# Attention over the heads of a token: groups of 32 tokens at a step of four instead of eight neighbours

## The chip, the cores and the metric

The kernel runs on one core of a Trainium2 chip. The metric is the device time of one launch in microseconds (us), the median of several runs. Lower is better. Engines are called as in the profile: PE (matrix products; PEld is its weight load), DVE (vector), ACT (activations), POOL, and SP, which here only issues transfers. Each engine works through its own list of instructions in order and waits on semaphores.

## The reference

One layer over x of shape (2, 4096, 512), in float32, with two halves that are both residual.

```python
h = layernorm(x);  k = h @ Wk.T;  r = h @ Wr.T
y = wkv_scan(-exp(time_decay), time_first, k, r)      # a recurrence over the 4096 tokens
x = x + (sigmoid(r) * y) @ Wo.T
z = layernorm(x)                                      # the feed-forward half works on z
h = rmsnorm(z, gamma1)
q = (h @ Wq + bq).reshape(b, t, 16, 32)
k, v = split(((h @ Wdown + bdown) @ Wup + bup).reshape(b, t, 16, 64))
att = softmax(einsum('bthd,btgd->bthg', q, k) / sqrt(32))   # 16 x 16 for each token
z = z + einsum('bthg,btgd->bthd', att, v).reshape(b, t, 512) @ Wo + bo
h2 = rmsnorm(z, gamma2);  gate = softmax(h2 @ Wg + bg)      # 8 experts, all of them used
x = x + z + einsum('btd,edf,bte->btf', h2, We, gate)
```

The attention here is unusual: it runs over the 16 heads within one token, not over tokens. Each token has a 16 x 16 matrix of scores of its own.

## The kernel before

**Tiles and stages.** The tokens are worked through in 32 tiles of T = 256. Four stages run at once on different tiles: "pre" (load and normalise tile i + 1), "mix" (the recurrence, tile i), "att" (the attention, tile i - 1) and "moe" (the experts, tile i - 2). One iteration runs a step of each. The order of the steps is a list written out by hand, `ORDER`, and each engine takes from it the steps in which it has work, in that order. Waits between engines are semaphore counts, kept in tables (`Steps`).

**Numbers.** A float32 operand is split into two float16 halves, "hi" and "lo", and a product is three float16 passes. For q and k, ACT makes the value and its hi half (`heads`, L595 and L598), POOL the lo half (`lo_half`, L476).

**Groups.** A matmul computes the scores of eight tokens at once: a group of NJ = 8 tokens gives 128 columns, 16 heads by 8 tokens. There are G = 32 groups in a tile. In the product of the group's q with its k only those entries count in which both columns belong to one token. Rows of a mask, added to the contraction, push the other entries far down, so that an exponential makes them zero.

**The stack.** For this product the parts of q and k are stacked along the partitions: 32 rows of head channels for each of three hi/lo pairings, eight mask rows, and in qs two more rows for the maximum (hi and lo). qs and ks have the shape [128, 32 groups, 4, 32] in float16: within a group 4 head blocks f by (4 blocks b times 8 tokens j). qo16 and k16 hold the 16 heads as 128 partitions (4 blocks f of 32) by 4 blocks b, so stacking moves data between partitions. SP does most of it by transfers inside the SBUF (L413, L417 in `att_up`): eight for q hi, four for q lo, four for k lo, of 32 partitions by 32 groups by 64 bytes each. DVE copies the two k hi parts in eight copies (L943 in `att_stack`).

```python
sp.dma_start(dst[n * HD:(n + 1) * HD, :, f, :],
             grouped(src, 0)[f * HD:(f + 1) * HD].rearrange("p g b j -> p g (b j)"))
```

**The steps around it, in `ORDER`.** `att_up` (K and V products, L1165; DVE writes V at L935), the recurrence's decay, `att_stack`, MoE step 2, `att_vt` (a transpose of V, L949), MoE 3, `att_max` (for each four groups four matmuls, L1182, and one reduce, L954, into four columns of mcol), with MoE 4 and 5 between, then `att_m`: the maxima, one per row of a group's matrix. They are needed as a row of the stack, so DVE turns mcol by a 32 x 32 block transpose (L959), makes hi and lo in m16 (L961, L799), and SP sends m16 in eight transfers into two rows of qs (L424): four for hi, four for lo, of 32 partitions by 64 bytes each.

```python
for l, step in enumerate(("m_hi", "m_lo")):
    sp.wait_ge(*att_dve.done(t, step))
    for f in range(F):
        sp.dma_start(qs[SCAN_ROWS + l:SCAN_ROWS + l + 1, :, f, :], m16[f * G:(f + 1) * G, l, :])
```

MoE 6 and 7 and half of the recurrence's end stand between this and `att_scores` (L1191), which waits on PE for all eight. ACT exponentiates (L608), `att_probs` multiplies by V (L1201), DVE divides. `att_back` turns the result back by one DVE transpose of 1,024 columns (L975), ACT and DVE split it (L614, L799), and after MoE 12 and 13 PE multiplies it by Wo (`att_project`).

Of the kernel before, what the change touches and what calls it, by code (L numbers as in the profile page):

```python
# [33 lines left out]
HF = CB // 2  # L34
F = H // CB
XS = 2048.0
NEG_INF = -1e38
# [111 lines left out]
def build(nc, x, wk, wr, wo1, decay, first, gamma1, wq, bq, wdown, bdown, wup, bup, wo2, bo, gamma2,  # L149
          wg, bg, we, ident_in, kmask_in, qmask_in, out):  # L150
    with ExitStack() as ctx:
# [61 lines left out]
        vp = sb("vp", [P, G, HD + 1])  # L213
        qs, ks = sb("qs", [P, G, F, CB * NJ], F16), sb("ks", [P, G, F, CB * NJ], F16)
        pr = sb("pr", [P, 2, 4 * P])
        mcol, mturn, m16 = sb("mcol", [P, G]), sb("mturn", [P, CB * NJ]), sb("m16", [P, 2, CB * NJ], F16)
        rden = sb("rden", [P, G])
# [13 lines left out]
        def grouped(split16, half_):  # L231

            return split16[:, half_, :, :].rearrange("p b t -> p (b t)").rearrange("p (g b j) -> p g b j", g=G, b=CB)

        def as_f32(flat):
            return flat.bitcast(F32).rearrange("p (b c) -> p b c", c=C)

        home = {"k": [as_f32(qs[:, :, :, :].rearrange("p g f x -> p (g f x)"))],
                "r": [as_f32(ks[:, :, :, :].rearrange("p g f x -> p (g f x)"))]}
        for name, after in zip(BIG[2:], BIG[3:]):  # L240
# [18 lines left out]
        def turned(n):  # L259
# [12 lines left out]
        stack_in = Steps(sem("stack_in"), 16, qk=16)  # L272
        m_in = Steps(sem("m_in"), 16, m=2 * F)
        stored = Steps(sem("stored"), 16, out=1)
# [14 lines left out]
        att_dve = Steps(sem("att_dve"), stats=2, idle=1, aggr=2, var=2, h=2, h_lo=2, xn=2, c_lo=1, v=4, stack=8,  # L289
                        vt=1, smax=8, m_turn=1, m_hi=1, m_lo=1, norm=16, ot=1, ot_lo=2, x2=2, h2=2, h2_lo=2)  # L290
        gate_dve = Steps(sem("gate_dve"), gl=1, gmax=1, gsub=1, gsum=1, grec=1, gmul=1, gates=1)
# [64 lines left out]
        def _(sp):  # L356
# [28 lines left out]
            def rest():  # L385

                for e in range(E):
                    load_weight(f"e{e}")
                sp.wait_ge(lo_done, split_done("r"))
                sp.dma_start(ks[3 * HD:SCAN_ROWS + 2, :, :, :], kmask_in.rearrange("a (g f x) -> a g f x", f=F, g=G)).then_inc(masks_in, 16)  # L390
                sp.dma_start(qs[3 * HD:SCAN_ROWS, :, :, :], qmask_in.rearrange("a (g f x) -> a g f x", f=F, g=G)).then_inc(masks_in, 16)

# [11 lines left out]
            def att_up(t, _):  # L404


                for src, dst, name, first in ((qo16, qs, "q", (0, 1)), (k16, ks, "k", ())):
                    rest = 2 if first else 1
                    for f in range(4):
                        for n in first:  # L410
                            if f == 0 and n == 0:
                                sp.wait_ge(*att_act.done(t, name))
                            sp.dma_start(dst[n * HD:(n + 1) * HD, :, f, :],  # L413
                                         grouped(src, 0)[f * HD:(f + 1) * HD].rearrange("p g b j -> p g (b j)")).then_inc(stack_in.sem, 16)
                    sp.wait_ge(*att_pool.done(t, f"{name}_lo"))
                    for f in range(4):
                        sp.dma_start(dst[rest * HD:(rest + 1) * HD, :, f, :],  # L417
                                     grouped(src, 1)[f * HD:(f + 1) * HD].rearrange("p g b j -> p g (b j)")).then_inc(stack_in.sem, 16)

            def att_m(t, _):  # L420
                for l, step in enumerate(("m_hi", "m_lo")):
                    sp.wait_ge(*att_dve.done(t, step))
                    for f in range(F):
                        sp.dma_start(qs[SCAN_ROWS + l:SCAN_ROWS + l + 1, :, f, :], m16[f * G:(f + 1) * G, l, :]).then_inc(m_in.sem, 16)  # L424

# [9 lines left out]
        def _(pool):  # L435
# [37 lines left out]
            def lo_half(t, step, dst):  # L473
                for b in range(CB):
                    pool.wait_ge(*att_act.done(t, step, 2 * b + 1))
                    nc.gpsimd.tensor_tensor(grouped(dst, 1)[:, :, b, :], t32[:, b % 2, :].rearrange("p (g j) -> p g j", g=G),  # L476
                                            grouped(dst, 0)[:, :, b, :], ALU.subtract).then_inc(att_pool.sem, 1)
# [27 lines left out]
        def _(act):  # L505
# [81 lines left out]
            def heads(t, use, step, dst, scale, bias, lo, before):  # L587

                for b in range(CB):
                    act.wait_ge(*att_pe.done(t, f"{use}{b // 2}"))  # L590
                    if b >= 2:
                        act.wait_ge(*att_pool.done(t, lo, b - 2))
                    elif before:
                        act.wait_ge(*att_pool.done(t, before, b + 2))
                    nc.scalar.activation(t32[:, b % 2, :], att_bank[ATT_BANK[use, b // 2]][:, (b % 2) * T:(b % 2) * T + T],  # L595
                                         ACT.Identity, bias=bias[:, b:b + 1], scale=scale).then_inc(att_act.sem, 1)
                    act.wait_ge(*att_act.done(t, step, 2 * b))
                    nc.scalar.activation(grouped(dst, 0)[:, :, b, :], t32[:, b % 2, :].rearrange("p (g j) -> p g j", g=G), ACT.Copy)\  # L598
                        .then_inc(att_act.sem, 1)
# [44 lines left out]
        def _(dve):  # L644
# [293 lines left out]
            def att_stack(t, _):  # L938

                dve.wait_ge(*att_act.done(t, "k"))  # L940
                for f in range(4):
                    for n in (0, 2):
                        V.tensor_copy(ks[n * HD:(n + 1) * HD, :, f, :],  # L943
                                      grouped(k16, 0)[f * HD:(f + 1) * HD].rearrange("p g b j -> p g (b j)")).then_inc(att_dve.sem, 1)

# [94 lines left out]
        def _(pe):  # L1040
# [234 lines left out]
```

## Time and profile before

| | |
|---|---|
| median of 3 runs | 3334.51 us (3332.51 to 3334.67) |
| profiled execution, its own time | 3332.17 us |
| profiled execution, span of the trace | 3330.3 us |
| PE busy | 2887.2 us, 87% |
| DVE busy | 2476.6 us, 74% |
| ACT busy | 956.6 us, 29% |
| POOL busy | 686.1 us, 21% |
| transfers | 588,333 packets, 102.96 MB; 556,562 under 512 bytes |

The span is what the trace covers, the time of the execution lies 1.9 us above it. Busy time is an average over all stages, so it doesn't tell where an engine sets the pace. In the rows below, a row of the timeline gives start, duration, engine, line, operation, what is written and read, and in brackets how long the engine had been idle and what ended it.

### The profile page before, as it was taken

What the parts mean: (1) busy time and instruction counts of PE and PEld (TensorE: products, weight loads), DVE (VectorE), ACT (ScalarE), POOL (GpSimd) and SP (SyncE); (2) the same over time, 40 slices, a digit from 0 to 9 for tenths busy, and PEclk for the clock granted to TensorE, in tenths of its full rate; (3) what the DMA queues carried; (4) which work ended last, traced back from release to release, by engine and by line L of the source; (5) the groups of instructions that cost most, each with busy time, mean ns of one, the idle gap of its engine ahead of it and who ended that gap; (6) DMA issues with size and microseconds to landing.
All of it is one profiled execution on the core that took longest, in us unless ns stands there. A gap on an engine that the chain in (4) does not pass through costs nothing.

```text
span 3330.3 us, 53600 instructions
## 1 busy us (share of the span) xinstructions
PE 2887.2 (87%) x18864; PEld 1791.2 (54%) x18864; DVE 2476.6 (74%) x4548; ACT 956.6 (29%) x1823; POOL 686.1 (21%) x745
## 2 busy tenths in 40 slices
PE   2359999998888989989998898999889998999889
PEld 2235555554555655555564555555555555555544
DVE  5797777778777768777777777768777777877753
ACT  2243232322332322322331332232233232232320
POOL 0111222212122212222221222221222221212210
PEclk9669999999999999999999999999999999999999
DMA  6011111101111101111111111111111110111110
GB/s 192 15 24 20 33 33 26 30 24 33 20 33 27 33 20 33 20 33 26 33 27 26 20 33 30 29 26 27 27 26 33 27 33 20 32 21 33 26 20 13
DMA packets 588333, 102.96 MB, mean 31 GB/s; under 512 B 556562, under 2 KB 556690, under 8 KB 588050
## 3 DMA queue, kind: packets, MB, share of 16 engines
q1 hardware_dynamic: 588068, 99.40, 16.4%
q8 instruction: 170, 2.79, 0.4%
q14 instruction: 95, 0.78, 0.1%
HBM read 48.49 MB, written 16.78 MB: 20 GB/s over the span
## 4 chain that ended last, share of the span: by engine, by line
PE 62%; DVE 23%; issue 7%; SPq 5%; DMA 2%; ACT 0%; POOL 0%; DVEq 0%; ACTq 0%; POOLq 0%
PE bank L1049 49%; PE bank L1201 6%; DVE mcol L954 4%; SPq L424 4%; DVE zz L865 3%; PE bank L1079 3%; DVE ks L943 3%; DVE wkv L839 2%; PE bank L1191 2%; DMA qs<-m 2%; DVE acc L1028 1%; DVE wkv L827 1%; PE bank L1165 1%; DVE ht L935 1%; DVE zz L832 1%
## 5 line engine op out<-in xcount | busy, mean ns | idle before, releaser
L1049 PE MATMUL bank<-w_e,h2t 128*128 128x512 f16 x6144 | 1479.4, 398 | 19.1 <-DVE acc L1028 19.1
L1049 PEld LDWEIGHTS bank<-w_e,h2t 128*128 128x128 f16 x6144 | 617.9, 103 | 757.5 <-issue 123.1
L1028 DVE SCALAR_TENSOR_TENSOR acc<-bank,gates,acc 128x512 f32<-128x512 f32 x512 | 373.6, 737 | 164.7 <-PE bank L1049 163.6
L1201 PEld LDWEIGHTS bank<-vp,pr 128*128 128x128 f32 x2048 | 263.9, 197 | 24.0 <-DVE hrow L970 3.9
L1201 PE MATMUL bank<-vp,pr 128*128 128x33 f32 x2048 | 259.7, 275 | 3.8 <-ACT pr L608 2.7
L608 ACT ACTIVATE pr<-bank,col 128x512 f32<-128x512 f32 x256 | 171.9, 685 | 316.1 <-PE bank L1191 315.7
L865 DVE RECIPROCAL zz<-zz 128x256 f32<-128x256 f32 x128 | 219.1, 1733 | 46.8 <-POOL zz L462 46.8
L1049 PE MATMUL bank<-w_o,xo 128*128 128x512 f16 x768 | 174.3, 384 | 58.8 <-DVE xo L799 58.8
L455 POOL TENSOR_TENSOR e<-wkv 128x512 f32<-128x512 f32 x64 | 72.1, 1127 | 645.6 <-DVE wkv L827 645.6
L1191 PE MATMUL bank<-qs,ks 106*128 106x128 f16 x1024 | 104.5, 236 | 113.9 <-DMA qs<-m 113.9
L1182 PE MATMUL bank<-ks,qs 104*128 104x128 f16 x1024 | 90.8, 231 | 125.7 <-DMA ks<-k 65.7
L935 DVE TENSOR_SCALAR ht<-bank,col,bvcol 128x256 f32<-128x256 f32 x128 | 61.8, 539 | 162.2 <-PE bank L1165 162.2
L1049 PE MATMUL bank<-w_o,qo 128*128 128x512 f16 x768 | 173.6, 383 | 4.4 <-DVE qo L799 4.4
L1049 PE MATMUL bank<-xo,w_k 128*128 128x256 f16 x1536 | 174.4, 274 | 0.0
L1049 PE MATMUL bank<-xo,w_r 128*128 128x256 f16 x1536 | 172.9, 273 | 0.0
L1049 PE MATMUL bank<-ht,w_q 128*128 128x256 f16 x1536 | 172.9, 273 | 0.0
L487 POOL TENSOR_TENSOR ve<-msq,eps_rms 128x2 f32<-128x2 f32 x32 | 6.3, 196 | 767.6 <-ACT hrow L620 767.6
L1049 PEld LDWEIGHTS bank<-xo,w_k 128*128 128x128 f16 x1536 | 151.0, 98 | 18.0 <-DVE xo L799 0.2
L1049 PEld LDWEIGHTS bank<-xo,w_r 128*128 128x128 f16 x1536 | 150.3, 98 | 17.4
L1049 PEld LDWEIGHTS bank<-ht,w_q 128*128 128x128 f16 x1536 | 150.2, 98 | 17.5
L954 DVE TENSOR_REDUCE mcol<-bank 128x4 f32<-128x512 f32 x256 | 158.4, 681 | 1.4 <-PE bank L1182 1.4
L462 POOL TENSOR_TENSOR zz<-wkv,zz 128x512 f32<-128x512 f32 x64 | 80.9, 1264 | 359.6 <-DVE wkv L839 359.6
(177 smaller groups left out, 3918.1 us busy)
## 6 DMA issues: line engine op xcount, KB each, us to landing
qs<-qo SPq DMA_DIRECT2D x384, 64.0 KB, 3.0
xk<-in_attn_x SPq DMA_DIRECT2D x32, 512.0 KB, 3.9
x<-in_attn_x SPq DMA_DIRECT2D x32, 512.0 KB, 3.6
result<-acc SPq DMA_DIRECT2D x32, 512.0 KB, 2.8
ks<-k SPq DMA_DIRECT2D x128, 64.0 KB, 3.0
w_e<-in_ffn_We SPq DMA_DIRECT2D x7, 1024.0 KB, 13.8
qs<-m SPq DMA_DIRECT2D x256, 2.0 KB, 1.7
qs<-in_attn_Wk SPq DMA_DIRECT2D x1, 1024.0 KB, 5.5
```

What stands on the lines that cost most here:

```text
L424: sp.dma_start(qs[SCAN_ROWS + l:SCAN_ROWS + l + 1, :, f, :], m16[f * G:(f + 1) * G, l, :]).then_inc(m_in.sem, 16)
L608: nc.scalar.activation(pr[:, k % 2, :], att_bank[ATT_BANK["S", k]][:, :], ACT.Exp, scale=colof["soft"])\
L865: V.reciprocal(zz[:, c, :], zz[:, c, :]).then_inc(mix_dve.sem, 1)
L935: V.tensor_scalar(va32[:, :, b, :], att_bank[ATT_BANK["V", b // 2]][:, (b % 2) * T:(b % 2) * T + T] .rearrange("p (g j) -> p g j", g=G), c ...
L943: V.tensor_copy(ks[n * HD:(n + 1) * HD, :, f, :], grouped(k16, 0)[f * HD:(f + 1) * HD].rearrange("p g b j -> p g (b j)")).then_inc(att_dve ...
L954: V.tensor_reduce(mcol[:, 4 * k:4 * k + 4], att_bank[ATT_BANK["M", k]][:, :].rearrange("p (g x) -> p g x", g=4), AX, ALU.max).then_inc(att ...
L1028: V.scalar_tensor_tensor(out=acc[:, s, :], in0=moe_bank[u % 2][:, :], scalar=gates[:, s, e:e + 1], in1=acc[:, s, :], op0=ALU.mult, op1=ALU ...
L1049: ins = nc.tensor.matmul(dst, left(a), right(b), start=(n == 0), stop=(n == last))
L1079: ins = nc.tensor.transpose(banks[b][:, c * T + s * P:c * T + (s + 1) * P], rows_[:, s, (2 * b + c) * P:(2 * b + c + 1) * P], ident[:, :])
L1182: ins = nc.tensor.matmul(att_bank[ATT_BANK["M", k]][:, n * P:(n + 1) * P], group(qs, SCAN_ROWS, 4 * k + n), group(ks, SCAN_ROWS, 4 * k + n ...
L1191: ins = nc.tensor.matmul(att_bank[ATT_BANK["S", k]][:, n * P:(n + 1) * P], group(ks, SCAN_ROWS + 2, 4 * k + n), group(qs, SCAN_ROWS + 2, 4 ...
L1201: ins = nc.tensor.matmul(att_bank[ATT_BANK["PV", k]][:, n * (HD + 1):(n + 1) * (HD + 1)], pr[:, k % 2, n * P:(n + 1) * P], vp[:, 4 * k + n ...
```

## The change

A group now takes every fourth token of 32 instead of eight neighbours. The groups come in GQ = 8 blocks of 32 tokens, R = 4 groups to a block; token t is in block t // 32, and its group within the block is t % 4. qs and ks get the shape [128, 8 blocks, 4, 32, 4], in which the group's number within its block is the last index. So 32 neighbouring tokens of a block b lie together: a transfer for the stack writes 256 bytes at once, and DVE copies runs of 128 elements. A group's columns are then no longer neighbours: PE reads every fourth column of the stack (for weights and for moving data). The V product reads its tokens in the new order too, so that everything behind it is laid out as before up to `att_back`, whose transpose becomes four, with the results written four elements apart. For the maxima the four groups of a block stand next to each other in the stack, as they do in mcol: m16 is made from mcol without the transpose, and a transfer sends four neighbouring maxima (8 bytes) from each of 128 partitions. There are 8 transfers for hi and 8 for lo.

```diff
-        qs, ks = sb("qs", [P, G, F, CB * NJ], F16), sb("ks", [P, G, F, CB * NJ], F16)
+        qs, ks = sb("qs", [P, GQ, F, CB * NJ, R], F16), sb("ks", [P, GQ, F, CB * NJ, R], F16)
-        mcol, mturn, m16 = sb("mcol", [P, G]), sb("mturn", [P, CB * NJ]), sb("m16", [P, 2, CB * NJ], F16)
+        mcol, m16 = sb("mcol", [P, G]), sb("m16", [P, 2, G], F16)
...
-            return split16[:, half_, :, :].rearrange("p b t -> p (b t)").rearrange("p (g b j) -> p g b j", g=G, b=CB)
+            return split16[:, half_, :, :].rearrange("p b t -> p (b t)").rearrange("p (g b y) -> p g b y", g=GQ, b=CB)
...
-        m_in = Steps(sem("m_in"), 16, m=2 * F)
+        m_in = Steps(sem("m_in"), 16, m=2 * GQ)
...
-                            sp.dma_start(dst[n * HD:(n + 1) * HD, :, f, :],
-                                         grouped(src, 0)[f * HD:(f + 1) * HD].rearrange("p g b j -> p g (b j)")).then_inc(stack_in.sem, 16)
+                            sp.dma_start(dst[n * HD:(n + 1) * HD, :, f, :, :].rearrange("p g x r -> p g (x r)"),
+                                         grouped(src, 0)[f * HD:(f + 1) * HD].rearrange("p g b y -> p g (b y)")).then_inc(stack_in.sem, 16)
...
-                    for f in range(F):
-                        sp.dma_start(qs[SCAN_ROWS + l:SCAN_ROWS + l + 1, :, f, :], m16[f * G:(f + 1) * G, l, :]).then_inc(m_in.sem, 16)
+                    for g in range(GQ):
+                        sp.dma_start(qs[SCAN_ROWS + l:SCAN_ROWS + l + 1, g, :, :, :].rearrange("a f x r -> a (f x) r"),
+                                     m16[:, l, g * R:(g + 1) * R]).then_inc(m_in.sem, 16)
...
-                        V.tensor_copy(ks[n * HD:(n + 1) * HD, :, f, :],
-                                      grouped(k16, 0)[f * HD:(f + 1) * HD].rearrange("p g b j -> p g (b j)")).then_inc(att_dve.sem, 1)
+                        V.tensor_copy(ks[n * HD:(n + 1) * HD, :, f, :, :].rearrange("p g x r -> p g (x r)"),
+                                      grouped(k16, 0)[f * HD:(f + 1) * HD].rearrange("p g b y -> p g (b y)")).then_inc(att_dve.sem, 1)
...
-                V.transpose(mturn[:, :], mcol[:, :]).then_inc(att_dve.sem, 1)
-                dve.wait_ge(*att_dve.done(t, "m_turn"))
-                V.tensor_scalar(m16[:, 0, :], mturn[:, :], -2.0 ** -14, None, ALU.mult).then_inc(att_dve.sem, 1)
+                V.tensor_scalar(m16[:, 0, :], mcol[:, :], -2.0 ** -14, None, ALU.mult).then_inc(att_dve.sem, 1)
                 dve.wait_ge(*att_dve.done(t, "m_hi"))
-                lo(m16[:, 1, :], mturn[:, :], -2.0 ** -14, m16[:, 0, :]).then_inc(att_dve.sem, 1)
+                lo(m16[:, 1, :], mcol[:, :], -2.0 ** -14, m16[:, 0, :]).then_inc(att_dve.sem, 1)
...
-                V.transpose(ot32.rearrange("p b (g j) -> p g b j", g=G), on[:, :, :].rearrange("p g (b j) -> p g b j", b=CB)).then_inc(att_dve.sem, 1)
+                for r in range(R):
+                    V.transpose(ot32.rearrange("p b (g j r) -> p r g b j", g=GQ, r=R)[:, r],
+                                on[:, :, :].rearrange("p (g r) (b j) -> p r g b j", r=R, b=CB)[:, r]).then_inc(att_dve.sem, 1)
...
-                                                       w16["u"][:, a, blk * P:(blk + 1) * P], c16[:, :], start=(a == 0), stop=(a == 1))
+                                                       w16["u"][:, a, blk * P:(blk + 1) * P],
+                                                       c16[:, :] if use == "K" else c16[:, :].rearrange("p (g j r) -> p g r j", g=GQ, r=R),
+                                                       start=(a == 0), stop=(a == 1))
...
-                return stacked[0:n_rows, g, :, :].rearrange("p f x -> p (f x)")
+                return stacked[0:n_rows, g // R, :, :, g % R].rearrange("p f x -> p (f x)")
...
-    j = np.arange(H * T) % NJ
+    j = np.arange(H * T) // R % NJ
```

The diff leaves out the same renaming in the q lo and k lo transfers (L417), in `lo_half` and `heads`, and in the load of the masks.

## Rows read from the trace of the kernel before

**Rows 1.** The head of the page.

```profile
span 3330.3 us, 53600 instructions
```

**Rows 2.** Waits, PE: engine, line, who it waited for: total us, times, longest.

```profile
PE bank L1191 <- DMA qs<-m: 113.9, 32, 9.8
PE bank L1182 <- DMA ks<-k: 65.7, 32, 10.0
```

**Rows 3.** Timeline of PE, one steady tile, from the V product to the scores.

```profile
1660.50 1.06 PE L1182 MATMUL bank<-ks,qs 104*128 104x128 f16 x16 [1.93 <-DMA ks<-k]
...
1665.36 0.40 PE L1182 MATMUL bank<-ks,qs 104*128 104x128 f16 x4 [1.20 <-DVE mcol L954]
```

**Rows 4.** Timeline of DVE, the same tile.

```profile
1643.96 1.94 DVE L935 TENSOR_SCALAR ht<-bank,col,bvcol 128x256 f32<-128x256 f32 x4 [5.08 <-PE bank L1165]
...
1664.62 2.47 DVE L954 TENSOR_REDUCE mcol<-bank 128x4 f32<-128x512 f32 x4
...
1680.75 0.43 DVE L835 TENSOR_SCALAR zz<-zz 128x512 f32<-128x512 f32 x1
```

**Rows 5.** Chain of waits, first, a steady and last tile: start, duration, what.

```profile
298.64 3.72 PE bank L1049 x12
...
1670.18 0.22 DVE mturn L959
...
1670.43 0.19 DVE m L961
...
1675.04 1.79 DMA qs<-m
...
1676.95 1.03 PE bank L1191 x8
...
1681.53 0.81 PE bank L1201 x8
1682.34 0.23 PE bank L1191 x4
...
3245.05 5.06 PE bank L1049 x12
```

**Rows 6.** Timeline of SP's queue, the same steady tile.

```profile
1670.63 4.99 SPq L424 DMA_DIRECT2D qs<-m  x8
```

**Rows 7.** Instructions of a line: count, ns min/median/max, first and last start.

```profile
L424 SPq DMA_DIRECT2D qs<-m x256: 502/590/1349, 191.8 to 3242.2; - x128
...
L417 SPq DMA_DIRECT2D ks<-k x128: 593/672/1377, 172.9 to 3225.3; - x128
...
L372 SPq DMA_DIRECT2D bkcol<-in_ffn_bup x4: 432/432/507, 17.3 to 20.3; - x4
...
L391 SPq DMA_DIRECT2D qs<-in_qmask x1: 289/289/289, 52.3 to 52.3; - x1
...
L943 DVE COPY ks<-k x256: 415/419/1306, 168.9 to 3221.1; 32x1024 f16<-32x1024 f16 x128
```

**Rows 8.** Transfers: count, KB each, median us from issue to landing.

```profile
ks<-k SPq DMA_DIRECT2D x128, 64.0 KB, 3.0
...
bkcol<-in_ffn_bup SPq DMA_DIRECT2D x4, 0.5 KB, 1.8
```

**Rows 9.** Groups of instructions, 300 to 3100 us: busy us, mean ns.

```profile
L975 DVE STREAM_TRANSPOSE ht<-hrow 128x1024 f32<-128x1024 f32 x29 | 36.1, 1245 | 1.0
...
L856 DVE COPY carry<-wkv 128x6 f32<-128x6 f32 x57 | 8.8, 155 | 0.0
...
L959 DVE STREAM_TRANSPOSE mturn<-mcol 128x32 f32<-128x32 f32 x28 | 5.9, 212 | 1.0
```

**Rows 10.** Timeline, the way back and the projection of the steady tile.

```profile
1700.01 1.41 DVE L799 SCALAR_TENSOR_TENSOR qo<-ht,col,qo 128x512 f16<-128x512 f32 x2 [0.79 <-ACT qo L614]
...
1702.20 5.06 PEld L1049 LDWEIGHTS bank<-w_o,qo 128*128 128x128 f16 x24
```

**Rows 11.** Busy us by engine in a stretch, then PEclk, DMA share, GB/s.

```profile
1677.00:1678.00 1.00, 1.00 (x9) 0.93 (x10) 1.00 (x2) 0.41 (x1) 0.00 (x0) 0.50 0.00 0
```

More of the change, by code:

```diff
@@ L35 @@
 F = H // CB
+R = 4
+GQ = G // R
 XS = 2048.0
@@ L231, in grouped @@
         def grouped(split16, half_):
-            return split16[:, half_, :, :].rearrange("p b t -> p (b t)").rearrange("p (g b j) -> p g b j", g=G, b=CB)
+            return split16[:, half_, :, :].rearrange("p b t -> p (b t)").rearrange("p (g b y) -> p g b y", g=GQ, b=CB)
         def as_f32(flat):
             return flat.bitcast(F32).rearrange("p (b c) -> p b c", c=C)
-        home = {"k": [as_f32(qs[:, :, :, :].rearrange("p g f x -> p (g f x)"))],
-                "r": [as_f32(ks[:, :, :, :].rearrange("p g f x -> p (g f x)"))]}
+        home = {"k": [as_f32(qs[:, :, :, :, :].rearrange("p g f x r -> p (g f x r)"))],
+                "r": [as_f32(ks[:, :, :, :, :].rearrange("p g f x r -> p (g f x r)"))]}
         for name, after in zip(BIG[2:], BIG[3:]):
@@ L289, in build @@
         att_dve = Steps(sem("att_dve"), stats=2, idle=1, aggr=2, var=2, h=2, h_lo=2, xn=2, c_lo=1, v=4, stack=8,
-                        vt=1, smax=8, m_turn=1, m_hi=1, m_lo=1, norm=16, ot=1, ot_lo=2, x2=2, h2=2, h2_lo=2)
+                        vt=1, smax=8, m_hi=1, m_lo=1, norm=16, ot=R, ot_lo=2, x2=2, h2=2, h2_lo=2)
         gate_dve = Steps(sem("gate_dve"), gl=1, gmax=1, gsub=1, gsum=1, grec=1, gmul=1, gates=1)
@@ L389, in rest @@
                 sp.wait_ge(lo_done, split_done("r"))
-                sp.dma_start(ks[3 * HD:SCAN_ROWS + 2, :, :, :], kmask_in.rearrange("a (g f x) -> a g f x", f=F, g=G)).then_inc(masks_in, 16)
-                sp.dma_start(qs[3 * HD:SCAN_ROWS, :, :, :], qmask_in.rearrange("a (g f x) -> a g f x", f=F, g=G)).then_inc(masks_in, 16)
+                sp.dma_start(ks[3 * HD:SCAN_ROWS + 2, :, :, :, :].rearrange("a g f x r -> a (g f x r)"), kmask_in).then_inc(masks_in, 16)
+                sp.dma_start(qs[3 * HD:SCAN_ROWS, :, :, :, :].rearrange("a g f x r -> a (g f x r)"), qmask_in).then_inc(masks_in, 16)
             def pre_load(t, _):
@@ L412, in att_up @@
                                 sp.wait_ge(*att_act.done(t, name))
-                            sp.dma_start(dst[n * HD:(n + 1) * HD, :, f, :],
-                                         grouped(src, 0)[f * HD:(f + 1) * HD].rearrange("p g b j -> p g (b j)")).then_inc(stack_in.sem, 16)
+                            sp.dma_start(dst[n * HD:(n + 1) * HD, :, f, :, :].rearrange("p g x r -> p g (x r)"),
+                                         grouped(src, 0)[f * HD:(f + 1) * HD].rearrange("p g b y -> p g (b y)")).then_inc(stack_in.sem, 16)
                     sp.wait_ge(*att_pool.done(t, f"{name}_lo"))
                     for f in range(4):
-                        sp.dma_start(dst[rest * HD:(rest + 1) * HD, :, f, :],
-                                     grouped(src, 1)[f * HD:(f + 1) * HD].rearrange("p g b j -> p g (b j)")).then_inc(stack_in.sem, 16)
+                        sp.dma_start(dst[rest * HD:(rest + 1) * HD, :, f, :, :].rearrange("p g x r -> p g (x r)"),
+                                     grouped(src, 1)[f * HD:(f + 1) * HD].rearrange("p g b y -> p g (b y)")).then_inc(stack_in.sem, 16)
             def att_m(t, _):
@@ L475, in lo_half @@
                     pool.wait_ge(*att_act.done(t, step, 2 * b + 1))
-                    nc.gpsimd.tensor_tensor(grouped(dst, 1)[:, :, b, :], t32[:, b % 2, :].rearrange("p (g j) -> p g j", g=G),
+                    nc.gpsimd.tensor_tensor(grouped(dst, 1)[:, :, b, :], t32[:, b % 2, :].rearrange("p (g y) -> p g y", g=GQ),
                                             grouped(dst, 0)[:, :, b, :], ALU.subtract).then_inc(att_pool.sem, 1)
@@ L597, in heads @@
                     act.wait_ge(*att_act.done(t, step, 2 * b))
-                    nc.scalar.activation(grouped(dst, 0)[:, :, b, :], t32[:, b % 2, :].rearrange("p (g j) -> p g j", g=G), ACT.Copy)\
+                    nc.scalar.activation(grouped(dst, 0)[:, :, b, :], t32[:, b % 2, :].rearrange("p (g y) -> p g y", g=GQ), ACT.Copy)\
                         .then_inc(att_act.sem, 1)
```

## The prediction

> **What bounds the kernel now.** I read the views in this order: the page's head, the list of waits, the chain of waits over one steady tile, and then the timelines of PE, DVE and SP over that tile (one of 32, some 99 us each, in a span of 3330.3 us [rows 1]). The reader should see in the waits that PE, the busiest engine, waits in every tile for two transfers that the change touches: 32 times for the row of maxima (113.9 us in all, 3.56 a tile) and 32 times for the stack of k (65.7 us, 2.05 a tile) [rows 2]. A wait is only worth its length if nothing else would take its place, so both need the timelines.
>
> The stack: PE's first maxima matmuls start at 1660.50, after 1.93 us of waiting for the stack, but soon PE waits again, for DVE (1.20 us at 1665.36) [rows 3]. DVE has worked without a gap since 1643.96, when the V matmuls released it, and takes up the first maxima only at 1664.62 [rows 4]. Matmuls that had started earlier would have waited for it: the stack lies about 4 us beside the path. In this stretch DVE is the bound.
>
> The maxima: after the last reduce the path runs through the turn of the column (1670.18), two small DVE operations, the issues on SP's queue, and the last landing [rows 5]. SP takes 4.99 us for eight issues [rows 6], of which one has a median of 590 ns [rows 7]: from start to start (4.99 - 0.59) / 7 = 0.63 us, 0.04 of it a gap. The last issue starts at 1675.04, lands 1.79 us later, and 0.12 us after that PE starts the scores [rows 5]. From the first issue (1670.63) to the scores (1676.95) it is 6.32 us. Behind it the chain is PE's own, matmul after matmul, up to the next tile's V. So one period is: a PE-bound stretch, a DVE-bound one, and these 6.3 us in which SP's issuing sets the pace. Whatever lengthens them lengthens the tile.
>
> **The change, part by part.**
>
> *The maxima's transfers.* Eight of 64-byte pieces (32 each) become sixteen of 8-byte pieces (128 each). All sixteen are issued by SP, in one row, and the scores wait for all. An issue inside the SBUF took 590 ns (the maxima, 32 pieces) or 672 ns (the stack, 1,024 pieces) [rows 7]: it is the issue that costs and hardly the number of pieces, so I take the old pitch, 0.63 us. The last of sixteen starts 15 x 0.63 = 9.45 us after the first; with 1.79 and 0.12 the scores come 11.36 us after the first issue, where they came after 6.32: **+5.04 us**. Bounds of the pitch: 128 pieces of 4 bytes from outside the SBUF were issued in 432 ns [rows 7], a pitch of 0.48 with the old gap: 15 x 0.48 + 1.91 = 9.11, +2.79. The stack's 672 gives 0.71: 12.56, +6.24. The middle is the nearest row, with the same source, destination row and engine.
>
> The Trainium skill speaks against so dear an issue: "DMA: Bandwidth & Descriptors", section "Anatomy of one DMA", puts the sequencer's dispatch at about 50 ns and the rest of a small transfer's price at its completion. By that figure eight more issues would be an estimated 0.4 us a tile and the total would come out near 3339 us. The trace disagrees: 590 ns of SP for each [rows 7], back to back. The same page's rule to join many small transfers into one points as the trace does.
>
> *Their landing.* 128 pieces of 4 bytes landed in 1.8 us, the stack's 1,024 pieces of 64 bytes in 3.0 [rows 8]; the maxima's 32 in 1.79 [rows 5]. The new transfer is like the first of these in the number of its pieces and like the last in source and destination, so I keep 1.79, with 3.0 as the upper end (+39 us in all); none landed much sooner than 1.8, so there is no gain. What the rows don't show is 128 such pieces falling into one partition.
>
> *The turn.* The transpose of the column goes, and the two operations behind it read the column directly, in the same size: the path loses 1670.43 - 1670.18 = **-0.25 us** [rows 5].
>
> *The stack.* Sixteen transfers of 1,024 pieces become sixteen of 256. They may land up to 3.0 - 1.8 = 1.2 us sooner, and their issues may shorten, but PE would then wait for DVE instead, as it does at 1665.36: **0**. If that cover were gone, the whole wait of 65.7 us would be the gain. They can be 4 us later without harm, too.
>
> *DVE's eight copies of the k stack* are on the path. The sizes stay, the runs grow from 32 to 128 elements. A copy takes 419 ns [rows 7], the shortest copy here 155 [rows 9]: (419 - 155) / 1024 = 0.26 ns an element, where the transposes take (1245 - 212) / 992 = 1.04 ns [rows 9]. At a quarter of that the short runs show no cost, so I take **0**; the far end, every copy at 155 ns, would be 8 x 0.264 = 2.1 us a tile, 68 us in all. The ACT and POOL operations that write the split halves keep their sizes too, and they lie beside the DVE stretch: 0.
>
> *The way back.* One transpose of 1,024 elements becomes four of 256. From 212 ns for 32 elements and 1.04 ns for each further one [rows 9], each is 212 + 224 x 1.04 = 445 ns; four with three gaps of 0.03 are 1.87, against 1.245: +0.63 us. DVE is done with the low halves at 1700.01 + 1.41 = 1701.42, and PE comes to the projection at 1702.20, behind two MoE steps [rows 10]: 0.78 us of cover, so **0**, but only just. The new transposes write 4-byte elements 16 bytes apart. No row shows that; at twice the time an element they would be 4 x 678 ns and three gaps = 2.80, 1.56 more than before, 0.78 beyond the cover: +25 us.
>
> The Trainium skill ("SBUF — State Buffer", the note on cachelines) says that an access wants two hits in each line of 16 bytes to run at full rate. By that rule these writes, one hit a line, would slow and the time would be that +25 us; no row of this trace bears on it.
>
> *The matmuls that read with a step of four.* 32 pairs for the maxima, 32 for the scores, eight V matmuls a tile. Four pairs of scores took 0.23 us, 0.057 a pair [rows 5]; no row shows a stepped read. The nearest slower pace is that of the float32 pairs, 0.81 us for eight, 0.10 a pair [rows 5]: 32 x 0.045 = 1.4 us a tile, +46 us. The maxima would hide such a loss behind DVE's reduces; eight V matmuls, two columns to one of these, would pay 8 x 0.09 = 0.7 us ahead of the DVE stretch, +23. A gain has no reason, since a unit step is the plainest. I take **0**: the row of the same matmuls, in engine, size and type, is nearer than that of another type.
>
> *The clock.* PE's granted clock after the wait is 0.50, the lower level, 1.2 GHz [rows 11]. What that costs varies already: the twelve MoE matmuls behind the first scores take 3.72 us in the first and 5.06 in the last of the 20 tiles in which the chain shows them [rows 5]; 13 of the 20 take 3.5 to 4.1, seven 4.9 to 5.1. A wait of 9 instead of 4 us leaves the clock as low as it already is, so 0; if every tile went to 5.1 us it would be about 13/20 x 1.4 = 0.9 us, +29 in all.
>
> **Sum.** 5.04 - 0.25 = 4.79 us a tile, x 32 = 153 us. The profiled execution had a span of 3330.3 [rows 1] and a time of its own of 3332.2, 2.3 under the median of 3334.5; I add to the median: **3488 us, 4.6% slower**. SP has nothing else due in the added 5 us: DVE, the engine behind the next load, is occupied until 1680.75 [rows 4], when the sixteenth issue would just be out.
>
> **The rivals.**
> - *The new pieces and steps cost more than their issue* (0.22). The landing rises to 3.0 us (+39), or the stepped reads run at the float32 pace (+46, and +23 with V), or the transposes overrun (+25): 3513 to 3573 for one or two of them, 3621 with all; the transposes alone, 3513, have 0.05 of the chance. For: none of these forms is in the trace. Against: 4-byte pieces landed in 1.8 us.
> - *The issue is cheaper in its new form* (0.09), 0.48 a pitch: 2.79 - 0.25 = 2.54 a tile, 3416. For: 432 ns for 128 tiny pieces. Against: from SBUF to SBUF the medians are 590 and 672.
> - *The stack was on the path after all* (0.05): 65.7 us come back, 3422. For: PE's wait. Against: DVE's gapless stretch.
> - *Not slower* (0.07). The place is SP's queue between the maxima and the scores, the price one issue. Sixteen break even at 15p + 1.91 = 6.32 + 0.25, p = 0.31 us. The cheapest issue of the trace, 289 ns [rows 7], would without a gap give 15 x 0.289 + 1.91 = 6.25, -0.32 a tile, 3324. For: that row. Against: it moves eight long runs, and all 256 of the maxima's issues took at least 502 ns. The skill's figure for dispatch stands behind this rival as well; by it alone it would be the forecast.
>
> **How the numbers follow.** My forecast has 0.57. Its own range, pitch 0.58 to 0.71, is 3463 to 3526. The range for 8 in 10 is **3420 to 3575**: below lie the not-slower cases and some of the cheap issues, above the cases where several unknown costs meet. What a measurement of this kernel can tell from no change is about 0.2%, 7 us. Slower by more than that: 0.93; within: 0.03; faster: 0.04, the last two from the last rival.
>
> **What the changed profile would show.** SP's line of the maxima's transfers: 512 issues near 590 ns. PE's wait for the maxima: from 3.56 to about 8.4 us a tile, some 267 in all. Landing near 1.8 us. PE's waits for the stack smaller, those for DVE's reduces larger by as much. Pairs of scores still at 0.057, DVE's copies at 419, transposes near 445 without a PE wait at the projection. Wrong would be a pitch far from 0.63, a landing over 2.5 us, slower pairs, or a DVE stretch (1643.96 to 1670.2 here) that has become shorter or longer.

## The result, and the profile after

The changed kernel takes 3549.26 us, the median of four runs (3548.95 to 3552.88), beside 3333.51 for four runs of the kernel before (3330.87 to 3334.67) on the same chip: a ratio of 1.0651, interval 1.0632 to 1.0669. That is +215.8 us where +153 was forecast. The time lies inside the range of 3420 to 3575, but 61 us above the forecast and outside the likeliest case's own 3463 to 3526.

The head of the page, after, and from the list of PE's waits (total us, times, longest) the rows that answer to [rows 1, 2]:

```profile
span 3547.2 us, 53868 instructions
```

```profile
PE bank L1196 <- DMA qs<-m: 252.4, 32, 15.2
PE bank L1187 <- DVE mcol L957: 77.9, 31, 8.7
PE bank L1187 <- DMA ks<-k: 6.6, 1, 6.6
```

PE's wait for the maxima has grown from 3.56 to 252.4 / 32 = 7.89 us a tile. Its wait for the stack is almost gone, 65.7 to 6.6. Its wait for DVE's reduces is up to 77.9 us; in the same view before it is

```profile
PE bank L1182 <- DVE mcol L954: 59.7, 111, 5.6
```

So 59 us less of the one wait came back as only 18 more of the other; unit_reads below shows where the rest went. Next the chain of waits of one steady tile (start, duration, what), with the end of the same iteration:

```profile
1637.45 1.79 PE bank L1168 x12
...
1665.38 0.19 DVE m L962
...
1675.18 1.99 DMA qs<-m
...
1677.30 1.11 PE bank L1196 x8
1678.41 3.89 PE bank L1052 x12
1682.30 0.81 PE bank L1206 x8
1683.11 0.47 PE bank L1196 x4
...
1721.87 2.98 issue
1724.85 1.59 PE bank L1082 x8
1726.45 6.36 PE bank L1052 x24
```

The timelines of SP, DVE and PE in the same tile (start, duration, engine, line, operation; in brackets the idle time before it and what ended it):

```profile
1639.27 1.92 DVE L938 TENSOR_SCALAR ht<-bank,col,bvcol 128x256 f32<-128x256 f32 x4 [5.55 <-PE bank L1168]
...
1660.57 2.43 PE L1187 MATMUL bank<-ks,qs 104*128 104x128 f16 x16 [2.30 <-DVE mcol L957]
...
1665.59 10.19 SPq L426 DMA_DIRECT2D qs<-m  x16
...
1700.06 2.01 DVE L977 STREAM_TRANSPOSE ht<-hrow 128x256 f32<-128x256 f32 x4
...
1704.39 4.95 PEld L1052 LDWEIGHTS bank<-w_o,qo 128*128 128x128 f16 x24 [0.23 <-DVE qo L802]
```

From the first issue (1665.59) to the scores (1677.30) it is now 11.71 us, where it was 6.32. The stretch of DVE from V to the last reduce (1639.27 to 1665.38) is 26.11 us long, before 1643.96 to 1670.18 = 26.22 [rows 4, 5]: the stack gave nothing to the path in this tile. Now the scores. In the chain four pairs take 0.47 us, before 0.23 [rows 5]. The row of the V product takes 1.79 us; it holds twelve matmuls, the eight of K, which are still read with a unit step, and the first four of V. In the chain of before it is

```profile
1642.61 1.32 PE bank L1165 x12
```

Last, the instructions of a line (count, ns min/median/max, first and last start), after:

```profile
L426 SPq DMA_DIRECT2D qs<-m x512: 469/601/1042, 192.8 to 3456.8; - x171
...
L946 DVE COPY ks<-k x256: 407/418/1308, 171.0 to 3433.5; 32x1024 f16<-32x1024 f16 x128
...
L977 DVE STREAM_TRANSPOSE ht<-hrow x128: 596/619/644, 225.6 to 3483.1; 128x256 f32<-128x256 f32 x128
...
L1196 PEld LDWEIGHTS bank<-qs,ks x1024: 111/117/291, 204.7 to 3476.4; 106*128 106x128 f16 x171
L1196 PE MATMUL bank<-qs,ks x1024: 279/296/303, 204.7 to 3476.5; 106*128 106x128 f16 x171
```

and of the scores before:

```profile
L1191 PEld LDWEIGHTS bank<-qs,ks x1024: 95/101/291, 198.0 to 3261.4; 106*128 106x128 f16 x171
L1191 PE MATMUL bank<-qs,ks x1024: 217/218/314, 198.0 to 3261.5; 106*128 106x128 f16 x171
```

In the K and V products only V's moving data have a step, their weights have none; after, and the matmuls before:

```profile
L1168 PE MATMUL bank<-c,w_u x512: 272/328/409, 161.7 to 3426.6; 128*128 128x256 f16 x171
```

```profile
L1165 PE MATMUL bank<-c,w_u x512: 272/273/283, 160.8 to 3213.8; 128*128 128x256 f16 x171
```

Then the engines in the stretch behind the wait, after (columns as in [rows 11]):

```profile
1677.00:1678.00 1.00, 0.70 (x7) 0.71 (x8) 0.00 (x0) 0.03 (x1) 0.00 (x0) 0.50 0.37 55
```

So an issue costs 601 ns, as forecast. What the forecast lacks stands in the four lines of the scores: the same matmuls, as many and as large, take 296 ns instead of 218, and at full pace the chain shows 0.117 us a pair instead of 0.057.

### The profile page after: what moved, and what is told of

The parts are those of the page before. It is cut to its first block, busy times and chain, and to the rows that moved or that the text cites. A ratio compares the mean times of both kernels' runs of the same rounds, so it can differ in the third digit from the quotient of the medians.

```text
span 3547.2 us, 53868 instructions
## 1 busy us (share of the span) xinstructions
PE 3021.5 (85%) x18864; PEld 1892.1 (53%) x18864; DVE 2492.9 (70%) x4612; ACT 955.9 (27%) x1823; POOL 699.5 (20%) x745
## 4 chain that ended last, share of the span: by engine, by line
PE 60%; DVE 20%; SPq 9%; issue 8%; DMA 2%; ACT 0%; POOL 0%; DVEq 0%; ACTq 0%; POOLq 0%
PE bank L1052 46%; SPq L426 8%; PE bank L1206 6%; DVE mcol L957 3%; PE bank L1196 3%; DVE zz L868 3%; PE bank L1082 3%; DVE ks L946 3%; DMA qs<-m 2%; DVE acc L1031 2%; PE bank L1168 2%; DVE wkv L842 2%; DVE wkv L830 1%; DVE ht L938 1%; DVE zz L835 1%
## 5 line engine op out<-in xcount | busy, mean ns | idle before, releaser
L1052 PEld LDWEIGHTS bank<-w_e,h2t 128*128 128x128 f16 x6144 | 631.6, 104 | 766.9 <-issue 143.8
L1196 PE MATMUL bank<-qs,ks 106*128 106x128 f16 x1024 | 157.3, 294 | 252.4 <-DMA qs<-m 252.4
L1196 PEld LDWEIGHTS bank<-qs,ks 106*128 106x128 f16 x1024 | 113.2, 131 | 268.2 <-issue 212.5
L1187 PE MATMUL bank<-ks,qs 104*128 104x128 f16 x1024 | 143.2, 296 | 84.5 <-DVE mcol L957 77.9
L1187 PEld LDWEIGHTS bank<-ks,qs 104*128 104x128 f16 x1024 | 104.5, 120 | 130.7 <-DVE mcol L957 115.8
```

What stands on the lines that cost most here:

```text
L1052: ins = nc.tensor.matmul(dst, left(a), right(b), start=(n == 0), stop=(n == last))
L1187: ins = nc.tensor.matmul(att_bank[ATT_BANK["M", k]][:, n * P:(n + 1) * P], group(qs, SCAN_ROWS, 4 * k + n), group(ks, SCAN_ROWS, 4 * k + n ...
L1196: ins = nc.tensor.matmul(att_bank[ATT_BANK["S", k]][:, n * P:(n + 1) * P], group(ks, SCAN_ROWS + 2, 4 * k + n), group(qs, SCAN_ROWS + 2, 4 ...
```

## The experiments

The theory is A: the eight added issues make most of the time, and the stepped reads of PE the rest. Against it stands B, that the reads cost nothing on the path. The second group asks what part PE's clock after the longer wait has. The kernel before, run beside each group, took 3332.8 to 3334.7 us, so the times below compare directly to some 2 us.

### Issues, reads, queues, and a longer step

**unit_reads**: the changed kernel, but a group's 128 columns are read as neighbours.

```diff
-                return stacked[0:n_rows, g // R, :, :, g % R].rearrange("p f x -> p (f x)")
+                return stacked[0:n_rows, g // R, g % R, :, :].rearrange("p x r -> p (x r)")
```

> The changed kernel, but PE reads the 128 columns of a group for the maxima and the scores next to each other instead of every fourth one; the V product still reads in steps. The columns of four groups are mixed by this, so the output isn't the reference's. Theory A (of the 216 us, some 165 are the eight added issues with their landing, some 49 the stepped reads of the scores, some 15 those of V): four pairs of scores fall from 0.47 to 0.23 us, 24 such pairs and the first eight save 1.5 us a tile, 3549 - 49 = 3500 us. Theory B (the steps cost nothing on the path; what lies above the forecast is the landing of tiny pieces and contention): 3549 us, pairs unchanged.

3533.65 us, ratio 1.06 (1.0582 to 1.0618): 16 us less than the changed kernel, nearer to B. Yet the scores run as before; chain of waits, one steady tile and the end of its iteration:

```profile
1668.84 1.03 PE bank L1196 x8
1669.87 4.42 PE bank L1052 x12
...
1712.55 3.48 issue
1716.03 1.96 PE bank L1082 x8
1717.99 6.84 PE bank L1052 x24
```

The matmuls went back to 219 ns in the median, but other work of PE, not edited, got longer: the MoE step behind the scores, the transposes and the product at the iteration's end (1.59 and 6.36 in the changed kernel). Over the 31 tiles in which the chain shows it, the MoE step takes 4.68 us in the mean against 4.14: 17 us. The two at the iteration's end, which come so in the twelve tiles with this "issue" wait, are another (1.96 + 6.84) - (1.59 + 6.36) = 0.85 us, about 10 in all. PE's granted clock is lower there than in the changed kernel: 0.60 against 0.68 over the MoE step shown, 0.50 and 0.76 against 0.64 and 0.82 over the two rows at the end. This lower clock gave back most of what the reads had gained, so this run alone doesn't price the reads. PE's wait for the reduces is here 122.9 us, about 59.7 + 65.7: the old wait for the stack under another name. In the changed kernel the longer matmuls of the maxima fill 45 us of it.

**before_16_issues**: the kernel before, each transfer of the maxima cut into two of 16 pieces; nothing else.

```diff
...
-                        sp.dma_start(qs[SCAN_ROWS + l:SCAN_ROWS + l + 1, :, f, :], m16[f * G:(f + 1) * G, l, :]).then_inc(m_in.sem, 16)
+                        for n in range(2):
+                            sp.dma_start(qs[SCAN_ROWS + l:SCAN_ROWS + l + 1, n * 16:n * 16 + 16, f, :],
+                                         m16[f * G + n * 16:f * G + n * 16 + 16, l, :]).then_inc(m_in.sem, 16)
```

> The kernel before with its eight transfers of the maxima cut into sixteen of half the length (16 pieces of 64 bytes each), nothing else. Theory A: eight more issues at 0.63 us are 5.04 us a tile, 161 us, so 3334 + 161 = 3495 us, PE's wait for the maxima 3.6 + 5.0 = 8.6 us a tile. Theory B (the tiny pieces cost, not the number of issues): at most 20 us more than before.

3508.44 us, 1.0517 (1.05 to 1.0535): +174 for the issues alone, with pieces of the old kind, which land in 1.7 us. In the mean of the 32 tiles the way from the first issue to the scores is 11.29 us instead of 6.36, which is 158 of the 174; most of the rest lies behind it, where the first eight scores and the MoE step take 5.65 us together instead of 5.10. Most of the change's loss is in the issues.

**lo_half_from_act**: the changed kernel; ACT's queue issues the lo half's eight transfers, SP only the hi half's.

```diff
-                for l, step in enumerate(("m_hi", "m_lo")):
+                for l, step in enumerate(("m_hi",)):
...
+            def att_m(t, _):
+                act.wait_ge(*att_dve.done(t, "m_lo"))
+                for g in range(GQ):
+                    nc.scalar.dma_start(qs[SCAN_ROWS + 1:SCAN_ROWS + 2, g, :, :, :].rearrange("a f x r -> a (f x) r"),
+                                        m16[:, 1, g * R:(g + 1) * R]).then_inc(m_in.sem, 16)
...
```

> The changed kernel with the eight transfers of the lo half issued by ACT, which is idle there, beside SP's eight of the hi half. Theory A (SP issues one after another, and that is the pace): from the first issue to the scores 0.2 + 7 x 0.64 + 1.99 + 0.12 = 6.8 instead of 11.7 us, -4.9 us a tile, 3549 - 157 = 3392 us. Rival (the DMA engines or the one partition that takes all the pieces set the pace): landing grows as the issues come closer, and less than half of that is gained, above 3470 us.

3476.81 us, 1.0422 (1.0404 to 1.0439): 72 us less, where the theory that issues alone set the pace expected 157. Timeline of SP's queue, then the chain, then the instructions of ACT's line with its landing:

```profile
1538.46 5.04 SPq L426 DMA_DIRECT2D qs<-m  x8
```

```profile
1543.22 4.28 DMA qs<-m
1547.62 1.12 PE bank L1202 x8
```

```profile
L610 ACTq DMA_DIRECT2D qs<-m x256: 476/622/1581, 194.0 to 3385.3; - x128
...
DMA to landing us min/median/max: 2.2/4.2/5.0
```

Both queues issue at their old pace, but the landing rises from 2.0 to 4.2 us. From the first issue (1538.46) to the last landing (1547.50) it is 9.04 us; less one landing of 1.99, (9.04 - 1.99) / 15 = 0.47 us a transfer. The transfers are now limited by something behind the issue.

**step_of_32**: the changed kernel with R = 32: one block, 64-byte steps in PE's reads, two transfers of 128 pieces of 64 bytes for the maxima, one transpose back.

```diff
-R = 4
+R = 32
...
```

> The changed kernel with R = 32: a group takes every 32nd token of the tile, so the stack is read with a step of 64 bytes, a maxima transfer sends all 32 columns (64 bytes from each of 128 partitions), and there are two of them instead of sixteen; the transpose of the way back is one again. Theory A with reads that cost as much as at a step of 8 bytes (0.117 us a pair): from the first issue to the scores about 3 instead of 11.7 us, -8.7 us a tile, and some of the low clock behind the wait goes too: 3220 to 3275 us, faster than before. If the reads slow further with the step (0.2 us a pair or more), the maxima and scores pay 32 x 0.1 us each: 3350 to 3500 us.

3506.79 us, 1.0517 (1.0488 to 1.0546). A little more than the 3350 to 3500 expected for reads that slow further. PE and its weight loads hardly wait for the maxima any more (10.2 us in all), and the MoE step behind the scores runs in 2.59 us, yet the kernel is slow. Instructions of the scores' line:

```profile
L1195 PEld LDWEIGHTS bank<-qs,ks x1024: 135/153/310, 196.5 to 3437.8; 106*128 106x128 f16 x171
L1195 PE MATMUL bank<-qs,ks x1024: 379/407/428, 196.5 to 3438.0; 106*128 106x128 f16 x171
```

With the step the matmul goes from 218 over 296 to 407 ns and the weight load from 101 over 117 to 153. Eight pairs take 1.84 us in its chain, 0.23 a pair, four times the unit step's 0.057. The V product's matmuls, with a step on the moving side alone, start 0.430 us apart, where K's start 0.109 apart. The price of a stepped read is real and grows with the step.

### What PE's clock does in this

**after_filled_wait** and **before_filled_wait**: while PE waits for the maxima it does matmuls of 128 x 512 whose result is overwritten: 24 in the changed kernel, 12 in the kernel before.

```diff
             def att_scores(t, k):
+                att_free(t, "S", k)
                 if k == 0:
+                    for _ in range(24):
+                        nc.tensor.matmul(att_bank[ATT_BANK["S", 0]][:, :], w16["k"][:, 0, 0, 0:P], w16["r"][:, 0, 0, :], start=True, stop=True)
                     pe.wait_ge(*m_in.done(t, "m"))
-                att_free(t, "S", k)
```

> The changed kernel with 24 more matmuls of 512 columns on PE, in the wait for the maxima, written into the bank that the first scores overwrite. They are added work that changes nothing in the output. Theory: the wait leaves PE's clock at 1.2 GHz for the first scores and the MoE step behind them (1.11 and 4.14 us on average, where a MoE step takes 2.59 at full clock), and the fill of 5.3 us into a wait of 7 keeps it up: up to 1.7 us a tile, 3549 - 55 = 3494 us. If the low clock has nothing to do with the wait: 3549 us or, where the fill delays the scores, a little more.

3533.21 us, 1.0594 (1.0573 to 1.0615). 24 do not fill the wait (89.4 us of it are left), and the MoE step is at 2.59 us in about a third of the tiles only. The time lies between the two that were expected.

> The kernel before with 12 such matmuls (2.65 us) in its shorter wait of 3.6 us. Same theory: first scores from 1.03 to 0.45 us, MoE step from 4.2 to 2.6, 2.2 us a tile, 3334 - 70 = 3264 us. If the clock isn't the wait's doing: 3334 us.

3277.14 us, 0.9837 (0.9816 to 0.9857): work without any use makes the kernel before 56 us faster. In its chain:

```profile
1555.10 0.62 PE bank L1193 x8
1555.72 2.59 PE bank L1049 x12
```

The first eight scores take 0.59 us in the mean of the tiles instead of 0.88, and the MoE step 2.59 in each instead of 3.5 to 5.1. From the first scores to the last product of `att_probs` a tile is 1.83 us shorter, 59 in all, which is the whole gain. The kernel before thus pays for its own wait in clock; what the changed kernel pays these two runs don't separate.

**before_lo_from_act**: the kernel before with its lo half issued by ACT, as above (four transfers).

> The kernel before with the four transfers of the lo half of the maxima issued by ACT. If SP's issue is the pace: from the first issue to the scores 0.2 + 3 x 0.63 + 1.79 + 0.12 = 4.0 instead of 6.3 us, -2.3 us a tile, 3260 us. If transfers of this kind complete no faster than one in 0.47 us, as the sixteen of the changed kernel did from two queues (9.04 us from the first issue to the last landing): 7 x 0.47 + 1.79 + 0.12 = 5.2 us, -1.1 us a tile, 3299 us.

3268.22 us, 0.9804 (0.978 to 0.9827): faster than both kernels. Timelines of the two queues and of PE:

```profile
1544.22 2.47 SPq L424 DMA_DIRECT2D qs<-m  x4
1544.45 2.54 ACTq L607 DMA_DIRECT2D qs<-m  x4
...
1548.33 0.62 PE L1196 MATMUL bank<-qs,ks 106*128 106x128 f16 x8 [2.01 <-DMA qs<-m]
```

From the first issue to the scores it is 4.11 us instead of 6.32, which is 2.21 x 32 = 71 us; 65 were gained.

**before_16_lo_from_act**: before_16_issues with its lo half from ACT, so sixteen transfers from two queues, of 16 pieces instead of the 128 of lo_half_from_act.

> The kernel before with sixteen transfers of 16 pieces of 64 bytes, the eight of the lo half issued by ACT. It tells what set the 0.47 us of a transfer in the changed kernel from two queues. If it is a price of each transfer: as there, landing grows to some 4 us, and of the 5 us a tile that a second queue could give back about half comes: 3508 - 80 = 3428 us. If it is the number of pieces (128 there, 16 here): landing stays near 1.8 us, 0.2 + 7 x 0.64 + 1.8 + 0.12 = 6.6 instead of 11.5 us, 3508 - 157 = 3351 us.

3343.15 us, 1.0031 (1.002 to 1.0041). The landing keeps its length:

```profile
L610 ACTq DMA_DIRECT2D qs<-m x256: 510/611/994, 193.1 to 3253.8; - x128
...
DMA to landing us min/median/max: 1.7/1.7/2.5
```

As many transfers, from the same two queues: so it is their 128 pieces of 8 bytes, not their number, that held lo_half_from_act at 0.47 us a transfer. Whether it is the number of pieces or that they are so short, the two runs don't separate.

### The reads with the clock held

**after_full_fill**: 34 instead of 24 added matmuls in the changed kernel. **unit_full_fill**: the same with the unit reads of above. **v_unit_full_fill**: the same with a unit step for the V product alone.

```diff
...
-                                                       c16[:, :] if use == "K" else c16[:, :].rearrange("p (g j r) -> p g r j", g=GQ, r=R),
+                                                       c16[:, :],
...
```

> The changed kernel with 34 added matmuls (7.3 us) in the wait for the maxima instead of 24, which left 2.8 us idle and the MoE step behind the scores at 4.28 us in most tiles. Theory: with the wait filled nearly whole the clock stays up in all tiles, MoE step 2.59 instead of 4.14, first scores 0.94 instead of 1.11 us: -1.7 us a tile, 3549 - 55 = 3494 us, if the fill doesn't make the scores later. If the idle 2.8 us weren't the cause: 3533 us, as with 24.

3544.46 us, 1.0635 (1.0618 to 1.0653). The MoE step takes 2.59 us in every tile, yet only 5 us are gained, where 55 or 16 were expected. From the first scores to the last product of `att_probs` a tile is 1.51 us shorter than in the changed kernel, but from there to the next V product it is 1.29 longer. Waits of PE, and the chain at the end of an iteration:

```profile
PE bank L1082 <- issue: 68.8, 24, 3.8
...
PE bank L1198 <- DMA qs<-m: 16.1, 18, 3.6
```

```profile
1502.88 2.92 issue
1505.81 0.87 PE bank L1082 x6
1506.68 2.16 issue
1508.84 0.69 PE bank L1082 x2
1509.53 7.44 PE bank L1052 x24
```

A wait for nothing that the profile shows ("issue") comes twice in each of the twelve tiles instead of once: 24 times and 68.8 us, where the changed kernel has 12 and 40.1. The run is a base for the next two, no gauge of what the clock costs the changed kernel.

> The same filled wait, and the maxima and scores read with a unit step (the groups mixed, as in the earlier run). The fill takes the clock out of the comparison. Theory: reading in steps costs 0.06 us for each of 32 pairs of scores, 1.9 us a tile, so 61 us less than the filled kernel with steps, near 3433 us; the 16 us that the unit step gave without the fill were this gain less what a lower clock took back. Rival (reading costs the path only what was measured): 16 us less than the filled kernel with steps.

3486.81 us, 1.0457 (1.0439 to 1.0474): 57.7 less than after_full_fill. Of this, 54 lie between the first scores and the last product of `att_probs`, 19.16 instead of 20.85 us a tile. Its "issue" wait is nearly the same:

```profile
PE bank L1187 <- DVE mcol L957: 116.6, 75, 8.8
...
PE bank L1082 <- issue: 67.3, 24, 3.7
```

> The same filled wait and stepped scores, but the V product reads its tokens next to each other (V's tokens in the wrong order, so the output isn't the reference's). Theory: the 12 products of K and the first half of V fall from 1.79 to 1.32 us, and as DVE starts behind them, 0.47 us a tile come off the path: 15 us less than the filled kernel with steps. Rival (DVE has slack there): no difference.

3535.96 us, 1.06 (1.0582 to 1.0617): 8.5 less, between the 15 expected and none. The product is 0.47 us a tile shorter, but part of that was lost again, 0.11 us a tile in the DVE stretch and 0.26 between `att_probs` and the next V product. With the clock held behind the scores (the MoE step takes 2.59 us in all 31 tiles of the chain, in unit_full_fill in 30), the stepped reads of the stack are worth 58 us and those of V 8.5. Theory A stands, B falls. The parts don't add up exactly: 174 + 58 + 8.5, less 8 for the turn, is 232, measured 216, and the issues were priced at another clock than the reads.

**lo_from_act_filled**: before_lo_from_act with eight added matmuls.

> The kernel before with the lo half of the maxima issued by ACT, and eight added matmuls (1.7 us) in the 2 us of wait that were left. Theory: the MoE step behind the first scores falls from 4.28 to 2.59 us in the tiles where the clock had dropped, 1.7 us a tile in most of them: 3268 - 40 = 3228 us, the fastest of all. If the clock drops for an earlier idle stretch instead: 3268 us.

3269.39 us (3253.6 to 3276.66), 0.9815 (0.9798 to 0.9831): no gain over before_lo_from_act, with runs that lie 23 us apart. The landing of the maxima stands in the kernel's chain of waits in none of the 32 tiles, in before_lo_from_act in 13 and in the kernel before in 31. Elsewhere the chain runs past the scores, through DVE's work on the recurrence, which would leave a faster PE little to give; this was not tested, and why the runs differ is open.

## Why the prediction was right and wrong

**The maxima's transfers: right.** Last issue 9.59 us after the first, forecast 9.45; before_16_issues, which adds nothing but issues, has 158 us of its 174 on this way, forecast 161. The 50 ns that the prediction sets against this price from the Trainium skill ("DMA: Bandwidth & Descriptors", "Anatomy of one DMA") stand there for transfers issued from GpSimd, not from SP, so they were no price for this issue.

**Landing: nearly.** 1.99 us in the chain against the 1.79 taken. Together with the pitch, the way from the first issue to the scores grew by 11.71 - 6.32 = 5.39 instead of 5.04: +11 us over all tiles. The 128 pieces were a limit near by: in lo_half_from_act, with issues from two queues, the pace was 0.47 us a transfer.

**Turn: right.** The rows of the turn and of its successor's start are gone from the chain; 0.25 us.

**Stack and copies: right.** 0 on the path. PE's wait moved from the stack to the reduces, but not "by as much": 59 us less, 18 more, because the longer matmuls of the maxima fill the rest (122.9 us of wait for the reduces in unit_reads). A copy takes 418 ns against 419.

**Way back: right in sum, not in size.** One transpose takes 619 ns where 445 was worked out, but the four overlap and take 2.01 us together, 0.14 more than the 1.87 forecast, and PE's weight load waits 0.23 us for what follows. The float32 writes with 16-byte steps are slower one by one than the rows' pace, but the +25 us of the far end were not paid. In step_of_32 the one transpose, which reads in order and writes 128 bytes apart, takes 1955 ns instead of 1245.

**The matmuls that read with a step of four: the step that failed.** It took 0, because the row of the same matmul was nearer than that of another type. A pair takes 0.117 us, above even the float32 pace of 0.10 that was the upper end. On the path this is 24 pairs by 0.060 = 1.44 us and 0.08 for the first eight (1.03 to 1.11, at the lower clock, where the step costs little), and 0.47 for V (1.32 to 1.79): 1.99 us a tile, 64 in all. The maxima's 32 pairs did hide behind the reduces, as that step said. The bound was too low as well, but the value was chosen at its bottom: 46 + 23 us at the float32 pace would have given 3557, 8 from what was measured. That this comes so close is chance: 0.045 us a pair was too little for 0.060, and all eight V matmuls were counted ahead of DVE's start, where only four lie, at 0.117 us each. It is the first rival, given 0.22, that came in, by its part on the reads. The range holds the result because it was widened for costs of this kind, not because the forecast had this one.

The moving side alone is enough for the loss: V's matmuls of 256 columns, whose weights have no step, start 0.227 us apart where K's start 0.109 apart, a doubling as in the scores.

For this read the Trainium skill ("SBUF — State Buffer", the note on cachelines) would have given 0 too: a step of 8 bytes leaves two hits in each line of 16, enough by its rule for the full rate. The trace disagrees: 296 ns against 218 for the matmul, 0.117 us against 0.057 for the pair. For the transposes' writes, one hit a line, the trace agrees in direction, 619 ns against 445.

**Clock: nearly right between the two kernels, partly by luck, and silent on what lay in it.** The MoE step behind the scores took 4.22 us in the mean of 31 tiles before, and 4.14 after. But before, the clock was not in every tile "as low as it already is": over the first eight scores the granted clock was 0.50 in 18 of 32 tiles before and in all 32 after, and they took 0.88 us in the mean before, 1.11 after. The 20 tiles of the prediction were not all in which the chain shows the step; there are 31. With the same longer wait the step takes 4.62 us in before_16_issues and 4.68 in unit_reads, so 4.14 was not a matter of course. Also, undoing one cost lets the clock take part of it back (unit_reads), and in the kernel before it hides 56 us that no part of the prediction spoke of.

**The sum.** (5.39 - 0.25 + 1.99 - 0.11 for the DVE stretch - 0.08 for the MoE step) x 32 = 222 us from the steady tile, measured 216. In the mean of all 32 tiles the stretches differ by 0.467 (V product), -0.443 (DVE stretch with the turn), 5.356 (first issue to scores) and 1.369 us (first scores to the last product of `att_probs`): 6.749 us, x 32 = 216. The clock's part in the last of these was only read off, not separated.

Left open: whether a stepped weight load adds to a pair's time (in the scores and maxima both sides have the step in every run here; no run has it on the weights alone).

## What to carry to other kernels

A layout that saves a step by having PE read with a step pays on every matmul, so price it on the engine that reads most often, and where no row shows such a read, don't take 0 because the instruction has the same name. On the path, count transfers before bytes: eight more issues cost 174 us, and giving half of eight to a second queue brought 65. An experiment that takes work away on one engine can be masked by that engine's clock; hold the clock the same in both runs, then compare.

## What the runs showed that was not expected

- Filling PE's wait with twelve useless matmuls made the kernel before faster by 1.6%, 3277 us. Behind the idle wait the granted clock is at the lower level, 0.50 or 1.2 GHz, before [rows 11] and after (the row shown above); with the wait filled the MoE step takes 2.59 us instead of 3.5 to 5.1.
- Issues from two queues run side by side: 4.99 us for eight became 2.5 us for four on each. The Trainium skill ("DMA: Bandwidth & Descriptors", "Issuing engines are not separate DMA queues") says that this saves only the sequencer's time to start a DMA, usually little. Here it is that time which sets the pace, and it is worth 65 us of 3333.
- Transfers of 128 pieces of 8 bytes into one partition issued from two queues finished no faster than one in 0.47 us; those of 16 pieces of 64 bytes landed in 1.7 us at the same rate of issue.
- PE's "issue" wait at the iteration's end, 41.2 us in 12 waits before, doubled to 24 waits and 68.8 us when 34 matmuls were added to each iteration, but not with 24 (39.7 us, 12 waits). Its cause was not tested.
